# A Perceiver block with a 14-expert layer on one core: the order of turned rows, first output and block list between routing and the expert loop

## What is computed

```python
def _L0_ffn_ref(h, gate_w, w1, b1, w2, b2):      # 512 tokens, E = 14, F = 1024
    logits = x @ gate_w.T
    probs = jax.nn.softmax(logits, axis=-1)
    top2_p, top2_i = jax.lax.top_k(probs, 2)
    w = top2_p / jnp.maximum(top2_p.sum(-1, keepdims=True), 1e-10)
    hh = jnp.einsum('nd,edf->nef', x, w1) + b1
    hh = jax.nn.gelu(hh, approximate=False)
    all_out = jnp.einsum('nef,efd->ned', hh, w2) + b2
    out0 = all_out[n, top2_i[:, 0]]
    out1 = all_out[n, top2_i[:, 1]]
    moe_out = w[:, 0:1] * out0 + w[:, 1:2] * out1
    result = jnp.clip(x + moe_out, -100.0, 100.0).reshape(Bb, Ss, Dd)
```

## Time and profile before

| | us |
|---|---|
| median of 3 runs | 430.87 (430.41 to 431.71) |
| the profiled execution, whole | 432.17 |
| its span, first to last instruction | 430.6 |
| PE busy in the span | 413.9 (96%) |
| DVE busy | 329.9 (77%) |
| ACT busy | 216.3 (50%) |
| POOL busy | 62.4 (14%) |

### The profile page before, as it was taken

One profiled execution on the slowest core, in us unless ns is written; L12 is line 12 of the kernel. 1 busy time (PEld: TensorE's weight loads), 2 busy tenths in 40 slices (PEclk: granted clock), 3 DMA queues, 4 the chain that ended last, 5 costly groups with the idle time before them and its releaser, 6 DMA issues.

```text
span 430.6 us, 8283 instructions
## 1 busy us (share of the span) xinstructions
PE 413.9 (96%) x3102; PEld 313.1 (73%) x3102; DVE 329.9 (77%) x599; ACT 216.3 (50%) x374; POOL 62.4 (14%) x84
## 2 busy tenths in 40 slices
PE   7699999999999999999989979999999999999995
PEld 3276665688898799995668745787777778777783
DVE  4458789866249883438977989899988888988656
ACT  5265225121447343122436333698778888778410
POOL 5050000000404120102102801000000000000162
PEclk9899999999999999999999999999999999999999
DMA  7999699899960360009224579899999999994662
GB/s 250 391 342 361 246 430 370 325 408 407 418 264 3 89 279 2 2 2 374 118 84 164 195 234 362 312 348 371 385 396 380 363 376 378 348 359 195 224 192 98
DMA packets 24558, 116.74 MB, mean 271 GB/s; under 512 B 2838, under 2 KB 2854, under 8 KB 18000
## 3 DMA queue, kind: packets, MB, share of 16 engines
q1 hardware_dynamic: 12992, 93.33, 56.5%
q10 hardware_dynamic: 9328, 18.09, 10.9%
q0 software_dynamic: 2208, 4.91, 3.9%
HBM read 94.04 MB, written 21.23 MB: 268 GB/s over the span
## 4 chain that ended last, share of the span: by engine, by line
PE 81%; DVE 7%; DMA 5%; ACT 2%; POOL 2%; issue 2%; SPq 0%; ACTq 0%; DVEq 0%
PE banks L2053 5%; PE banks L2051 5%; PE banks L2052 5%; PE banks L2084 4%; PE banks L1633 4%; PE banks L1657 4%; PE banks L2095 3%; PE banks L2094 3%; PE banks L2093 3%; PE banks L1698 3%; PE banks L1658 3%; PE banks L1661 3%; DMA A<-in_ctxT 3%; PE banks L1772 3%; PE banks L1617 3%; PE banks L1782 3%
## 5 line engine op out<-in xcount | busy, mean ns | idle before, releaser
L1400 DVE TENSOR_TENSOR w_lo<-w,w_hi 128x1024 fp32r<-128x1024 f32 x48 | 55.5, 1218 | 0.0
L682 ACT ACTIVATE w_hi<-w 128x1024 fp32r<-128x1024 f32 x48 | 47.3, 1094 | 2.3 <-DMA w<-in_w 2.3
L767 ACT ACTIVATE A<-banks,b_sb 128x128 f32<-128x128 f32 x112 | 30.4, 383 | 25.9 <-PE banks L2064 16.3
L2051 PE MATMUL banks<-w_hi,cT_r 128*128 128x512 f32 x100 | 40.1, 401 | 0.0
L2053 PE MATMUL banks<-w_hi,cT_r 128*128 128x512 f32 x100 | 39.0, 390 | 0.0
L2052 PE MATMUL banks<-w_lo,cT_r 128*128 128x512 f32 x100 | 39.0, 390 | 0.0
L923 POOL DMA_DIRECT2D b_sb<-in_b1T x12 | 6.5, 541 | 135.6 <-ACT A L767 120.2
L1503 DVE COPY A<-banks 128x512 f32<-128x512 f32 x28 | 18.0, 685 | 10.2 <-PE banks L2053 10.2
L881 POOL TENSOR_TENSOR A<-A,hrec 128x1024 f32<-128x1024 f32 x8 | 16.5, 2056 | 61.0 <-DVE hrec L1218 61.0
L1209 DVE TENSOR_REDUCE hmax<-banks 128x16 f32<-128x1024 f32 x8 | 9.8, 1221 | 18.2 <-PE banks L1847 18.2
L2053 PEld LDWEIGHTS banks<-w_hi,cT_r 128*128 128x128 f32 x100 | 18.8, 188 | 4.0
(11 more groups left out here) (370 smaller groups left out, 1048.0 us busy)
## 6 DMA issues: line engine op xcount, KB each, us to landing
w<-in_w SPq DMA_DIRECT2D x24, 2048.0 KB, 7.8
rows_dram<-A ACTq DMA_DIRECT2D x1, 14592.0 KB, 51.2
A<-in_ctxT SPq DMA_DIRECT2D x8, 1024.0 KB, 10.3
A<-in_ctx SPq DMA_DIRECT2D x8, 1024.0 KB, 8.8
w<-in_w SPq DMA_DIRECT2D x5, 1024.0 KB, 8.1
w<-in_wlT SPq DMA_DIRECT2D x3, 1024.0 KB, 15.7
wqkv<-in_wqkvT SPq DMA_DIRECT2D x1, 3072.0 KB, 15.0
w<-in_convT SPq DMA_DIRECT2D x1, 3072.0 KB, 13.7
```

The source lines that it names most:

```text
L682: nc.scalar.activation(w1_hi[:, u, k * F:(k + 1) * F], w1[:, u, k * F:(k + 1) * F], ACT.Copy).then_inc(hi_ready, 1)
L767: ins = nc.scalar.activation(hT[:, u, f, :], HT[f // 4][:, tile(f % 4)], ACT.Gelu, bias=b1_sb[:, u, f:f + 1])
L1400: nc.vector.tensor_tensor(w1_lo[:, u, part], w1[:, u, part], w1_hi[:, u, part].bitcast(F32), ALU.subtract).then_inc(lo_ready, 1)
L2051: mm(HP[u][c][:, :], xr[:, 0, u, k, :], high[:, at], start=(i == 0), stop=False)
```

## The change

Three things move, and one scratch area with them:

1. On PE, `turn_x(2, 0)` no longer stands in the middle of `output(0, 0)` but behind it.
2. On DVE, `take_y(0, 0)` goes ahead of `take_xT(2, 0)` and `list_blocks`; `find_last` and `last_places` go behind the loop, ahead of line 1581. On ACT, `gelu(1, 1)` goes ahead of `store_first(0, 0)`.
3. The scratch areas `bm` and `bv` of `list_blocks` move from columns 4096 and 4608 of `A2`, which lie in the area that `gelu(1, 1)` writes, to columns 6144 and 6656.

```diff
-        bm, bv = (A2[:, at:at + OVER * E * MORE].rearrange("p (o i) -> p o i", o=OVER) for at in (4096, 4608))
+        bm, bv = (A2[:, at:at + OVER * E * MORE].rearrange("p (o i) -> p o i", o=OVER) for at in (6144, 6656))
...
             act.wait_ge(scattered, 16 * 2 * NT)
+            gelu(1, 1, 16, True)
             store_first(0, 0)
-            gelu(1, 1, 16, True)
...
             split_lo(2, 0, range(2), 2)
+            take_y(0, 0, 1)
             take_xT(2, 0)
             list_blocks()
-            take_y(0, 0, 1)
-            find_last()
-            last_places()
             take_h(2, 0)
...
             last = dve.value_load(pairs_i[0:1, 1:2], min_val=E // 2 - 1, max_val=MAX_BLOCKS // 2 - 1)
 
+            find_last()
+            last_places()
             dve.wait_ge(y_psum, 2 * last + 2)
...
-            output(0, 0, 16, lambda: turn_x(2, 0, 16))
+            output(0, 0, 16)
+            turn_x(2, 0, 16)
             turn_hidden(1)
```

## The result

| kernel | median us | runs | ratio to before (95% interval) |
|---|---|---|---|
| before | 430.87 | 11 | |
| after, first comparison | 428.56 | 11 | 0.9935 (0.9915 to 0.9956) |
| after, second comparison | 428.93 | 12 | 0.9957 (0.9933 to 0.9981) |
| after, third comparison | 428.72 | 12 | 0.9961 (0.9933 to 0.9989) |

The change makes the kernel faster. By the first comparison it is worth 2.8 us (1.9 to 3.7), where 1.7 was forecast; the time by that ratio, 430.87 x 0.9935 = 428.1 us, lies just under the range that was given (428.3). The two later comparisons say 1.9 and 1.7 us. The ratio is not that of the medians or of the means of the first comparison: those differ by 2.3 and 2.5 us, inside the range.

The account below looks back on a forecast made before the run. PE was taken to bound the kernel, its loop unchanged. Ahead of the loop 2.18 + 0.32 - 0.76 = 1.74 us, say 1.7, would go, with 0 behind it: 430.87 to 429.2 us, range 428.3 to 430.9.

Parts of the forecast that it names:

- The first wait: PE's 2.18 us idle in the first output, for the DMA of block 2's rows, would be covered by output work.
- The new wait of 0.76 us: Ahead of `hidden(2, 0)`, PE would wait 0.76 us for DVE's turned rows, copied behind the first output.
- The gelu: On ACT, `gelu(1, 1)` would start at 255.1 instead of 261.36, ending PE's 0.32 us wait before block 1's output.
- The term of 0.32 us: PE's idle time ahead of block 1's output, waiting for ACT's gelu, counted as a gain of 0.32 us.
- The store: On ACT, the first output's store would be issued behind the gelu, at 257.3, no later than before.
- DVE up to the loop: Between routing and loop, DVE would finish at 268.7, ahead of block 1's output ending at 269.0, and not hold PE.
- The pair count 1.3 us later: DVE's `list_blocks` would run 255.72 to 261.42, giving the pair count 1.3 us later, needed only at about 273.
- `w2` earlier: Ahead of the loop, block 2's `w2` would be issued at about 254.6 instead of 256.53.
- the loop at 12.6 us: The expert loop, bound by PE, would keep its length of 12.6 us per block.
- Behind the loop, 0: `find_last` and `last_places`, 3.59 us on DVE ahead of line 1581, would cost 0 there; bounds, a loss of 0 to 1.8.
- rival that lived on this sharing: Behind the loop, beside line 1581: late gathers, median 430.9, chance 0.10; or DVE held, 431.9, chance 0.05.
- The range: Whole kernel's median from 428.3, just under the largest gain, to 430.9, no gain, leaving out the slower case.

Follow-up runs that it names:

- c2: The changed kernel with DVE taking the turned rows of block 2 ahead of the first output's copy; ratio to before 0.995.
- c3: The kernel before with only `find_last` and `last_places` moved behind the loop; ratio to before 1.0007.
- c1: The changed kernel with `find_last` and `last_places` put back ahead of the loop, behind `list_blocks`; ratio to before 1.0044.
- c0: The kernel before, unedited, run and profiled a second time; ratio to before 1.0003.
- c7: The kernel before with ten matmuls of zeros filling PE's wait for the rows of block 2; ratio to before 1.0.
- e0: The kernel before with ten matmuls of zeros filling PE's wait for block 2's rows, run again; ratio to before 1.0021.
- c6: The changed kernel with `turn_x(2)` ahead of the last of the first output's eight matmuls, and DVE taking turned rows before the output's copy; ratio to before 0.993.
- c4: The kernel before with only block 1's gelu moved ahead of the store on ACT, and the scratch areas moved; ratio to before 1.0001.
- d0: The changed kernel again, unedited, in the second comparison; ratio to before 0.9957.
- d1: The late-turn version of c6 run again, against the changed kernel's order of transposes and DVE copies; ratio to before 0.9922.
- c5: The kernel before with only PE's `turn_x(2)` moved behind the first output, DVE and ACT in the old order; ratio to before 1.0056.

## Why the prediction was right or wrong, point by point

- **The first wait goes, covered by the output.** Right. No wait on L1617, in any of the three profiles after.
- **The new wait of 0.76 us.** Right: 0.80, released by L1417. `hidden(2)` starts 1.36 us sooner; 1.3 to 1.4 was read. But its cause was told in part only. c2 shows that without the copy ahead of it 0.64 us of it stay.
- **The gelu.** The term of 0.32 us was too small: the output of block 1 starts 1.79 us sooner, so the step is worth 0.43, and 0.10 more at its end, since a stream of matmuls that starts behind a wait is shown as 7.13 us and one that goes on as 7.03. The idle time in the earlier trace rows leaves out the overlap that the wait destroys. The store did not wait for the gelu to end, as I had it: it was issued at 253.40, while the gelu ran.
- **DVE up to the loop.** This is the step of the path that failed, beside the size of the gelu's term. I wrote that DVE was a little behind PE here before, and gave it no term: L2130 was held 0.2 us. With that the sum is 1.36 + 0.43 + 0.10 + 0.20 = 2.1 us instead of 1.7. And I wrote that the move of `find_last` is worth nothing by itself and that DVE would be about as close behind PE without it. The first half is borne out as far as c3 goes (1.0007, with a clock drop in its profile). The second is wrong (c1, 1.0044). Counted from the first output, DVE ends block 3's low part 0.7 us later in c1 than before, while PE could take the next step 1.9 us sooner than before; with the 0.2 us by which DVE was late already, PE loses 2.80 us there.
- **The pair count 1.3 us later, `w2` earlier, the loop at 12.6 us.** Right: `list_blocks` starts 1.2 us later and `w2` is issued 2.0 us sooner, counted from the first output. The rows of the loop, answering to the earlier trace rows:

```profile
286.15:298.73 12.58, 12.58 (x59) 9.87 (x58) 11.52 (x13) 10.55 (x19) 0.54 (x1) 1.00 0.96 375
...
374.25:386.84 12.59, 12.59 (x59) 9.86 (x58) 11.39 (x12) 10.25 (x18) 0.54 (x1) 1.00 0.92 353
```

- **Behind the loop, 0.** Right. DVE, POOL and PE there, answering to the earlier trace rows:

```profile
404.51 2.30 DVE L1581 TENSOR_SCALAR c_raw<-before,lpos,lw 128x128 f32<-128x128 f32 x8
...
404.55 0.97 POOL L931 DMA_INDIRECT wqkv<-rows_dram,slot_i  x1 [0.30 <-issue]
405.82 0.94 POOL L931 DMA_INDIRECT wqkv<-rows_dram,slot_i  x1 [0.30 <-issue]
...
406.14 0.60 PE L2151 MATMUL banks<-ident,c_raw 128*128 128x128 f32 x4
...
406.57 0.68 DVE L1541 COPY A<-banks 128x512 f32<-128x512 f32 x1
...
420.22 0.69 DVE L1596 TENSOR_TENSOR wqkv<-banks,cn 128x512 f32<-128x512 f32 x1 [0.57 <-PE banks L2176]
```

  Line 1581 takes 2.30 us instead of 2.13, and the issues beside it 0.97 and 0.94. PE's L2151 has no wait, and DVE's L1596 waits for PE and for no gather. So neither rival that lived on this sharing came about. By the Trainium skill's "SBUF — State Buffer", section "Who interferes with whom", tensor_scalar can enter a mode in which it keeps GpSimd from writing descriptors, if its operands meet certain conditions; these rows don't show it.
- **The range, and the clock without a term.** It allowed gains from 0 to 2.5 us, all read from one trace, and took the spread of executions as some tenths; the granted clock had no term. c0 shows 1.2 us between two profiles of one kernel on this stretch, mostly from the clock, and the three comparisons of the change give 1.7 to 2.8. The path gives 2.1, well inside the range. The first comparison went beyond it with executions that had more clock than usual: a mean of 0.9967 in those 11 of the changed kernel, with 5 of them at 1.000 and none under 0.992. The 107 of the kernel before have 0.9945, and within either kernel 0.01 less goes with 2.6 to 2.9 us more. So I estimate some 0.6 us for the 0.0022, and with the path that is 2.7. The clocks of the 11 executions before in that comparison are not on record, and whether the change itself raises the clock stays open: over all executions the difference is 0.0014 with a standard error of 0.0007, c7 and e0 found nothing, and the two later comparisons gave 1.9 and 1.7. That these meet the forecast is luck in part, since the path is worth 2.1.

## What to carry to other kernels

An engine with a slack of a few tenths of a us behind the bottleneck becomes the bottleneck as soon as that one is sped up: before summing the waits that an edit removes, shift the bottleneck's timeline by the gain and look who is late then. Here three of the edits gained nothing or lost when made alone, one kernel with all but one lost too, and together they gained 2.1 us. And a transfer's wait can be covered by splitting the work around it late. Here the split before the last piece was better than the one in the middle or behind the end, since both the landing and DVE's passes then lay under PE's work.

## What the runs showed of the hardware

- In the profiles, PE's granted clock fell to 0.50 behind idle times of 2.27, 2.43, 2.64 and 2.83 us around the change, and stayed at 1.00 behind ones of 1.99 and 2.18. Where it fell, 1.6 to 1.7 us were lost in the matmuls that followed. But the length of the idle time alone does not decide it. Ahead of L1633, early in the kernel, the clock fell behind 1.95 us in c6 and behind 2.36, 2.74, 2.88 and 3.52 in c4, d0, d1 and before, and it stayed up behind 2.35, 2.50, 2.69 and 2.97 in c2, c5, after and c0. In c3 it fell at 9.5 us with no idle time of over 1.59 us ahead of that. The 16 records took 5.35 us where it fell and 3.65 where it stayed:

```profile
13.72 5.35 PE L1633 MATMUL banks<-A 128*64 128x512 f32 x16 [1.95 <-DMA A<-in_ctxT]
```

```profile
15.20 3.65 PE L1633 MATMUL banks<-A 128*64 128x512 f32 x16 [2.97 <-DMA A<-in_ctxT]
```

  The first row is from c6, the second from c0.
- The 24 executions of a kernel that keeps PE busy in that time were no faster than 107 of the kernel before.
- The mean of a whole execution differs by more than 1% within one kernel (429.2 to 434.8 us for the kernel before), mostly with the mean granted clock (0.985 to 0.999). A comparison of twelve executions a side is sure to about 0.25%, and three of the same pair gave 0.9935, 0.9957 and 0.9961.
